# A hand-written interleaving of three pipelines: reciprocal before maximum on VectorE, and another order for TensorE's side work

## The chip, the cores and the metric

The kernel runs on 1 core of one Trainium2 chip. The metric is the device time of one execution in microseconds. Three runs of the kernel before took 1211.97 us in the median (1211.19 to 1215.45).

## The reference

The input is 8 sequences of 256 tokens with 256 channels, all in float32. Four layers follow one another, each with a residual and a layernorm (`x = _layernorm(x + layer(x))`):

- A: an operator with a long convolution. q, k and v are projected; q and k go through a depthwise convolution of 3 taps; `kv = k * v` is convolved over the sequence with `ssm_kernel` by FFT (here matrix products with a Fourier table); then `(y + kv * D_skip) * q` is projected.
- B: causal attention with 16 heads of 16 channels, whose output modulates a gated MLP of width 1024: `mod = 0.1 * tanh(attn @ A)`, `gate = silu(h @ W_in.T + mod * (h @ A) @ B)`, `mlp = gate * up @ W_down.T`.
- D: linear attention by a cumulative sum, `q * cumsum(k * v)`, and a projection.
- a mixture of 64 experts with 6 chosen per token, and a shared expert `silu(g) * u @ shared_down.T`. `topk` of the softmaxed router logits gives the weights.

The softmax of B is where the change is: for each head and each row of 256 scores the kernel takes the maximum, exponentiates with the sum collected on the way, takes the reciprocal of the sum, multiplies, and transposes the probabilities for the product with the values.

## The kernel before

The work has a first part, up to about 740 us, that runs the layers A, B and D (and the shared expert and the routing, called S and D4 to D6) over the 8 sequences, and then a loop over 133 chunks of 128 rows for the experts, and a last loop that adds the results up. The change touches only the first part.

That part is a software pipeline. In turn `it` layer A (and C, the preparation of B) works on sequence `it`, layer B on sequence `it - 1`, layer D on sequence `it - 2`, and the scattering of rows (G) on sequence `it - 3`. Each layer is cut into small parts with names, and a string of names (`TURN`, L313) gives their order. Every engine walks the same string in order and does its own share of each name, if it has one, so the string is the order of TensorE, VectorE, ScalarE and GpSimd at once. `TURN` is used in turns 0 and 2 to 7, `SECOND` in turn 1, `LAST_BUT_ONE` in turn 8 and `LAST` in turn 9. Semaphores alone hold the engines together; each engine is strictly in order.

Attention is cut into 12 units (0 to 3: four heads against 128 keys, 4 to 11: two heads against 256 keys). For unit u:

- TensorE's part `u` (L773) makes the scores of unit u (mask by L741, products by L744) into one of two banks, then transposes the probabilities of unit u-2 (`turn_probs`, L631, which waits for GpSimd's scaling of them and for ScalarE's copy of the transposes before), then multiplies those of u-3 with the values (L762; from unit 4 on two units together, L768, in every second part).
- VectorE's part (L1293) takes the maximum of unit u (L1301, wants the scores of u) and then the reciprocal of the sums of unit u-1 (L1307, wants the exponentials of u-1).
- ScalarE's part (L1012) exponentiates unit u (L1019, wants the maximum) and then copies the transposed probabilities of unit u-2 out of PSUM (L1025).
- GpSimd's part (L530) multiplies the probabilities of unit u-1 by the reciprocals (L537).

Between the units stand parts of A and D. Those the change moves: `A4b` (TensorE, L681, with L686: the second half of the inverse transform, 8 matmuls), `A4z` (VectorE, L1232: adds the skip term and multiplies by q, lines L1236 and L1243; it waits for A4b), `D3o` (VectorE, L1370: the layernorm's output x3, by L1163), `D4` (TensorE, L842: transposes x3 by L631, waits for D3o; ScalarE copies it out by L1063), `A5` (TensorE, L698: output projection of A, 8 matmuls by L626, waits for A4z), `A5n`, `A5o` (VectorE: residual, moments and output of A's layernorm), `S0` `S1` `S2` (TensorE L855/L864, ScalarE L1071/L1078, VectorE L1415/L1419 and L1422: the three tiles of the shared expert, each of which needs the one before to have left its PSUM bank), `SDa` and `SDb` (TensorE L883: the shared expert's output in two halves, both want S2's result), `SD` (VectorE L1451), `D4l` (TensorE L851: router logits), `D4m` (VectorE L1380 and ScalarE L1068), `A6n` (VectorE L1269 and L1272, GpSimd's root), `A6o` (VectorE L1277). In the trace x3 is named x_row. After unit 14 TensorE goes on with `B6c` (L787), the first instruction of a long stretch of MLP work.

Of the kernel before, what the change touches and what calls it, by code (L numbers as in the profile page):

```python
# [35 lines left out]
GROUPS = P // PAIR  # L36
# [85 lines left out]
def build(nc, d):  # L122
# [6 lines left out]
    with ExitStack() as ctx:  # L129
        def sb(name, shape, dt=F32):  # L130
            return ctx.enter_context(nc.sbuf_tensor(name, shape, dt))
# [64 lines left out]
        UNITS, PVS = GROUPS + 2 * GROUPS, 2 * GROUPS  # L196
        PROBS, PROBTS = 3, 4
        nmx, sums, rec = (sb(n, [P, UNITS, 4]) for n in ("nmx", "sums", "rec"))
# [77 lines left out]
        def need(eng, name, value):  # L276

            if isinstance(value, int) and value <= 0:
                return
            eng.wait_ge(S[name], value)  # L280
# [11 lines left out]
        class Chain:  # L292
# [17 lines left out]
                self.wait()  # L310


        TURN = """A1 A1b D1 A1q u0 D2k A1k u1 G0 D2x A2 u2 G1 D2v A3a u3 G2 A3b u4 G3 A3p D2q D2w u5 G4 D3 u6 G5 D3n A4a u7 G6 D3o D4 A4b A4z  # L313
            u8 G7 S0 u9 G8 A5 u10 G9 A5n D4l S1 u11 G10 A5o D4m S2 A6n u12 G11 SDa u13 A6o D4t SDb SD u14 B6a B6c B6b C1 f0 D4k f1 C2 f2 D5 f3 D5p C2v
            f4 D4w D5h f5 f6 f7 C2h B8 D6""".split()

        SECOND = """A1 A1b A1q A1k A2 A3a u0 A3b u1 A3p u2 u3 A4a u4 A4b A4z u5 u6 A5 u7 A5n u8 A5o u9 A6n u10 A6o u11 u12 u13 u14
# [10 lines left out]
        def turns(eng, parts):  # L328

            def turn(it, order=TURN):  # L330
                for name in order:
                    b = it - LAG[STAGE.get(name[0], name[0])]
                    if isinstance(b, int) and not 0 <= b < NB:
                        continue
                    if name in parts:
                        parts[name](b)
# [803 lines left out]
        def _(dve):  # L1140
# [152 lines left out]
            def unit(u):  # L1293
                w = P if u < GROUPS else L
                def part(b):
                    if u == 0:
                        cbn.start(b)
                    if u < UNITS:
                        dve.wait_ge(S["b_s"], b * UNITS + u + 1)
                        need(dve, "b_exp", (b - 1) * UNITS + u + 1)  # L1300
                        dve.tensor_reduce(nmx[:, u, 0:512 // w], bank[:, u % 2, :].rearrange("p (h k) -> p h k", k=w), AX, ALU.max,  # L1301
                                          negate=True).then_inc(S["b_max"], 1)
                    if u:
                        n = 4 if u - 1 < GROUPS else 2
                        dve.wait_ge(S["b_exp"], b * UNITS + u)
                        need(dve, "b_scaled", (b - 1) * UNITS + u)
                        dve.reciprocal(rec[:, u - 1, 0:n], sums[:, u - 1, 0:n]).then_inc(S["b_rec"], 1)  # L1307
                return part

            def B6(b):  # L1310
# [289 lines left out]
```

## Time and profile before

| | before |
|---|---|
| median of 3 runs | 1211.97 us (1211.19 to 1215.45) |
| the profiled execution's own time | 1210.18 us |
| its span | 1208.1 us |
| TensorE busy | 1030.5 us (85%) |
| VectorE busy | 690.0 us (57%) |
| GpSimd busy | 485.0 us (40%) |
| ScalarE busy | 360.7 us (30%) |

In a timeline a row gives the start in us, the time it took in us, the engine, the line, and what is written from what; in brackets stands how long the engine had been idle before it and what ended that. Matmuls overlap, so a row's end lies a little behind the next row's start. PE is TensorE, DVE is VectorE, ACT is ScalarE, POOL is GpSimd. Rows are merged where equal instructions follow one another (x8 are eight).

### The profile page before, as it was taken

To read this page: it belongs to the slowest core of one execution; us is meant where nothing else is said; L and a number is where in the kernel's file an instruction comes from. 1 tells how busy PE (TensorE), PEld (TensorE's weight loads), DVE (VectorE), ACT (ScalarE), POOL (GpSimd) and SP (SyncE) were. 2 spreads that over 40 slices of the span, in tenths; PEclk is the share of its full clock that TensorE was granted. 3 is DMA by queue.
4 is the path that set the end of the run, shared out by engine and by line. 5 is a ranking of instruction groups with operands and counts; after the bars stand their busy time and mean duration, and the time that the engine had idled before them with its cause. 6 is when DMAs were issued, how large, how long until landed. Compare 5 with 4: busy or idle time off the path is not lost. (4 is left out here: it accounts for less than half of the span.)

```text
span 1208.1 us, 23670 instructions
## 1 busy us (share of the span) xinstructions
PE 1030.5 (85%) x6301; PEld 841.4 (70%) x6301; DVE 690.0 (57%) x2250; ACT 360.7 (30%) x1114; POOL 485.0 (40%) x626
## 2 busy tenths in 40 slices
PE   5466798898998998997988888648999999999966
PEld 4344586776776776776866656537888888888955
DVE  1733455776765765675675646454555555555546
ACT  1024434344243243254253153001111111111243
POOL 0413224136245145154163152353555555555522
PEclk8778899999999999999999989968999999999989
DMA  9149950131220310410400410028999999999776
GB/s 363 62 101 290 286 124 1 40 88 37 75 62 31 90 45 35 104 32 31 104 29 25 104 37 19 29 92 268 308 307 309 306 302 302 306 291 310 263 259 245
DMA packets 129986, 184.67 MB, mean 153 GB/s; under 512 B 29749, under 2 KB 99989, under 8 KB 127517
## 3 DMA queue, kind: packets, MB, share of 16 engines
q1 hardware_dynamic: 94720, 104.41, 31.8%
q10 hardware_dynamic: 22989, 45.98, 11.0%
q0 software_dynamic: 12240, 33.83, 7.9%
q8 instruction: 18, 0.29, 0.1%
q14 instruction: 19, 0.16, 0.0%
HBM read 123.09 MB, written 61.60 MB: 153 GB/s over the span
## 5 line engine op out<-in xcount | busy, mean ns | idle before, releaser
L537 POOL TENSOR_TENSOR prob<-prob,rec 128x512 f32<-128x512 f32 x96 | 100.3, 1045 | 164.8 <-DVE rec L1307 163.4
L599 POOL DMA_INDIRECT y_rows<-sh_gu,ids x133 | 130.8, 984 | 60.2 <-POOL spare L290 56.8
L1019 ACT ACTIVATE prob<-bank,nmx 128x128 f32<-128x128 f32 (+1 forms) x256 | 104.9, 421 | 156.4 <-DVE nmx L1301 156.4
L1090 ACT ACTIVATE inv<-bank 88x256 f32<-88x256 f32 x159 | 60.3, 379 | 269.8 <-PE bank L929 269.8
L1523 DVE COPY sh_gu<-bank 128x256 f32<-128x256 f32 x133 | 56.4, 424 | 97.1 <-PE bank L938 96.8
L1301 DVE TENSOR_REDUCE nmx<-bank 128x2 f32<-128x512 f32 (+1 forms) x96 | 65.8, 686 | 77.4 <-PE bank L744 71.0
L938 PE MATMUL bank<-w_in,inv 88*128 88x256 f32 x428 | 109.8, 379 | 0.0
L631 PE MATMUL bank<-cst,prob 128*128 128x128 f32 x384 | 62.4, 287 | 39.3 <-ACT probT L1025 20.5
L562 POOL DMA_INDIRECT x_rows<-x_copy,desti x84 | 87.4, 1041 | 15.7 <-issue 15.7
L631 PEld LDWEIGHTS bank<-cst,prob 128*128 128x128 f32 x384 | 43.8, 146 | 55.3 <-POOL prob L537 50.6
L938 PEld LDWEIGHTS bank<-w_in,inv 88*128 88x128 f32 x428 | 72.7, 190 | 6.0
L802 PE MATMUL bank<-h2T,w_up 128*128 128x256 f32 x256 | 66.4, 382 | 0.0
L1025 ACT ACTIVATE probT<-bank 128x512 f32<-128x512 f32 x96 | 57.4, 598 | 28.8 <-PE bank L631 28.8
L804 PE MATMUL bank<-h2T,w_in 128*128 128x256 f32 x256 | 65.7, 379 | 0.0
L290 POOL TENSOR_TENSOR spare<-ones_row 128x1 f32<-128x1 f32 x168 | 31.1, 185 | 83.9 <-DVE sh_gu L1523 66.4
L815 PE MATMUL bank<-w_down,actT 128*128 128x256 f32 x256 | 60.0, 385 | 0.9
L929 PE MATMUL bank<-fwd,w_up 128*88 128x128 f32 x432 | 58.4, 279 | 2.4 <-DVE fwd L1505 1.5
L552 POOL TENSOR_TENSOR products<-z,products 128x512 bf16<-128x512 f32 x8 | 9.2, 1152 | 126.9 <-ACT products L1006 126.9
L929 PE MATMUL bank<-fwd,w_down 128*88 128x128 f32 x416 | 54.9, 275 | 2.4 <-DMA w_in<-in_e_w 1.3
L929 PE MATMUL bank<-inv,w_down 128*88 128x128 f32 x424 | 55.7, 274 | 1.0 <-DMA w_in<-in_e_w 0.3
L815 PEld LDWEIGHTS bank<-w_down,actT 128*128 128x128 f32 x256 | 46.8, 190 | 12.7 <-DVE actT L1329 6.3
L1046 ACT ACTIVATE gt<-bank 128x256 f32<-128x256 f32 x64 | 24.5, 383 | 104.0 <-PE bank L807 81.4
(264 smaller groups left out, 2300.0 us busy)
## 6 DMA issues: line engine op xcount, KB each, us to landing
w_in<-in_e_w ACTq DMA_DIRECT2D x107, 176.0 KB
w_down<-in_e_w SPq DMA_DIRECT2D x105, 176.0 KB
x_rows<-sgt SPq DMA_DIRECT2D x2, 8192.0 KB, 36.8
fwd<-x_rows SPq DMA_DIRECT2D x78, 132.0 KB
w_up<-in_e_w SPq DMA_DIRECT2D x54, 176.0 KB
w_up<-in_e_w ACTq DMA_DIRECT2D x52, 176.0 KB
w_down<-x_rows SPq DMA_DIRECT2D x54, 132.0 KB
stack_q<-q_parts SPq DMA_DIRECT2D x16, 384.0 KB, 6.0
```

Of the source, the lines that this page charges most:

```text
L537: pool.tensor_tensor(p, p, r, ALU.mult).then_inc(S["b_scaled"], 1)
L562: pool.indirect_dma_start(x_rows, bass.IndirectOffsetOnAxis(ap=desti[:, n:n + 1].bitcast(U32), axis=0), rows[:, n // TOPK, :], None).then_ ...
L599: pool.indirect_dma_start(y_rows, bass.IndirectOffsetOnAxis(ap=ids[s][:].bitcast(U32), axis=0), yc[s], None).then_inc(S[f"m_st{s}"], 16)
L631: return pe.transpose(out, x, ident)
L802: pe.matmul(psum(n, L, 2 * L), w_up[:, kt, cols], h2T[:, kt, :], start=(kt == 0), stop=(kt == KT - 1))
L804: pe.matmul(psum(n, 0, L), w_in[:, kt, cols], h2T[:, kt, :], start=(kt == 0), stop=False)
L815: mm = pe.matmul(psum(1, tt * D, (tt + 1) * D), actT[:, f, tt * P:(tt + 1) * P], w_down[:, f, :], start=(f == 0), stop=(f == FT - 1))
L929: mm = pe.matmul(bank[0:IH, 3 + n, m * P:(m + 1) * P], w1[s][:, kt, m * IH:(m + 1) * IH], xcT[n][:, kt, :], start=(kt == 0), stop=(kt == K ...
L938: mm = pe.matmul(psum(6 + c.slot(2), 0, D), hs[n][:, m, :], w2[s][:, m, :], start=(m == 0), stop=(m == 1))
L1019: i = act.activation(prob[:, u % PROBS, h * w:(h + 1) * w], psum(u % 2, h * w, (h + 1) * w), ACT.Exp, bias=nmx[:, u, h:h + 1], accum_out=s ...
L1090: act.activation(hs[n], bank[0:IH, 3 + n, 0:2 * P].rearrange("p (a b) -> p a b", a=2), ACT.Silu).then_inc(S["m_hs"], 1)
L1301: dve.tensor_reduce(nmx[:, u, 0:512 // w], bank[:, u % 2, :].rearrange("p (h k) -> p h k", k=w), AX, ALU.max, negate=True).then_inc(S["b_m ...
```

## The change

Two edits. In VectorE's part of a unit the reciprocal of unit u-1 now comes before the maximum of unit u. And in `TURN`, from unit 7 on, the side work stands in another order: A4b goes ahead of D4, D4 moves behind unit 8 and stands with A5, S0 moves behind unit 9, and SDa moves behind unit 13; VectorE's D3o now comes after A4z, and its A5n, A5o, D4m and A6n each come before the S part that they had followed. The other three orders stay.

```diff
-        TURN = """... A4a u7 G6 D3o D4 A4b A4z
-            u8 G7 S0 u9 G8 A5 u10 G9 A5n D4l S1 u11 G10 A5o D4m S2 A6n u12 G11 SDa u13 A6o D4t SDb SD u14 B6a ...
+        TURN = """... A4a u7 G6 A4b A4z D3o
+            u8 G7 D4 A5 u9 G8 A5n S0 u10 G9 D4l A5o S1 u11 G10 D4m A6n S2 u12 G11 A6o D4t u13 SDa u14 SDb SD B6a ...
@@ VectorE's unit(u) @@
+                    if u:
+                        n = 4 if u - 1 < GROUPS else 2
+                        dve.wait_ge(S["b_exp"], b * UNITS + u)
+                        need(dve, "b_scaled", (b - 1) * UNITS + u)
+                        dve.reciprocal(rec[:, u - 1, 0:n], sums[:, u - 1, 0:n]).then_inc(S["b_rec"], 1)
                     if u < UNITS:
                         dve.wait_ge(S["b_s"], b * UNITS + u + 1)
                         need(dve, "b_exp", (b - 1) * UNITS + u + 1)
                         dve.tensor_reduce(nmx[:, u, 0:512 // w], ...).then_inc(S["b_max"], 1)
-                    if u:
-                        ... (the same five lines)
```

## Rows read from the trace of the kernel before

**Rows 1.** The page: the span, and busy time with its share by engine.
```profile
span 1208.1 us, 23670 instructions
PE 1030.5 (85%) x6301; PEld 841.4 (70%) x6301; DVE 690.0 (57%) x2250; ACT 360.7 (30%) x1114; POOL 485.0 (40%) x626
```

**Rows 2.** Busy time by stretch: three TURN turns, each from L787 to L787.
```profile
core 0: us, PE busy (x) PEld busy (x) DVE busy (x) ACT busy (x) POOL busy (x), PEclk, DMA share, GB/s
221.24:307.21 85.97, 77.32 (x488) 61.58 (x484) 57.35 (x164) 34.02 (x109) 35.21 (x36) 1.00 0.23 60
...
483.57:570.51 86.94, 78.00 (x487) 61.34 (x483) 57.84 (x164) 34.01 (x109) 34.99 (x35) 1.00 0.22 58
570.51:659.18 88.67, 79.70 (x488) 62.49 (x484) 57.87 (x164) 34.01 (x109) 34.97 (x35) 0.98 0.20 54
```

**Rows 3.** Timeline of TensorE in a turn at full clock, unit 7 to B6c.
```profile
279.89 0.60 PE L631 MATMUL bank<-cst,prob 128*128 128x128 f32 x4
282.61 0.66 PE L631 MATMUL bank<-cst,x_row 128*128 128x128 f32 x4 [2.12 <-DVE x_row L1163]
283.10 1.89 PE L686 MATMUL bank<-inv,products 128*128 128x256 f32 x8
284.83 0.27 PE L741 MATMUL bank<-csb 128*128 128x256 bf16 x1
...
286.26 1.99 PE L864 MATMUL bank<-x3T,sh_gu 128*128 128x256 f32 x8
...
289.08 0.63 PE L631 MATMUL bank<-cst,prob 128*128 128x128 f32 x4 [0.49 <-ACT probT L1025]
...
292.40 0.63 PE L631 MATMUL bank<-cst,prob 128*128 128x128 f32 x4 [0.64 <-ACT probT L1025]
...
297.80 1.97 PE L864 MATMUL bank<-x3T,sh_gu 128*96 128x256 f32 x8 [0.62 <-DVE sact L1422]
300.04 0.63 PE L631 MATMUL bank<-cst,prob 128*128 128x128 f32 x4 [0.26 <-ACT probT L1025]
...
302.04 1.56 PE L883 MATMUL bank<-sh_dn,sact 128*128 128x256 f32 x6 [0.80 <-DVE sact L1422]
304.75 0.66 PE L631 MATMUL bank<-cst,prob 128*128 128x128 f32 x4 [1.15 <-POOL prob L537]
...
307.21 1.13 PE L787 MATMUL bank<-h2T,b_a 128*128 128x256 f32 x4
```

**Rows 4.** Timeline of VectorE in the same stretch.
```profile
280.95 1.61 DVE L1163 TENSOR_SCALAR x_row<-d_kv,mvD,yD 128x256 f32<-128x256 f32 x2
285.04 0.87 DVE L1236 SCALAR_TENSOR_TENSOR kv<-kv,vec,bank 128x256 f32<-128x256 f32 x2 [2.48 <-PE bank L686]
...
286.71 0.68 DVE L1301 TENSOR_REDUCE nmx<-bank 128x2 f32<-128x512 f32 x1
...
302.78 0.17 DVE L1307 RECIPROCAL rec<-sums 128x2 f32<-128x2 f32 x1
```

**Rows 5.** Timeline of GpSimd in the same stretch.
```profile
303.66 1.03 POOL L537 TENSOR_TENSOR prob<-prob,rec 128x512 f32<-128x512 f32 x1
```

**Rows 6.** Busy time by stretch, just behind D4's wait in two turns.
```profile
282.61:286.02 3.41, 3.41 (x31) 2.92 (x35) 0.87 (x2) 0.60 (x1) 0.68 (x1) 1.00 0.13 43
370.49:373.90 3.41, 3.41 (x11) 2.53 (x10) 0.57 (x2) 0.46 (x1) 0.00 (x0) 0.50 0.11 40
```

**Rows 7.** Timeline of TensorE in a turn with half clock: unit 9's transposes.
```profile
465.31 0.60 PE L631 MATMUL bank<-cst,prob 128*128 128x128 f32 x4
```

**Rows 8.** The tile rec: what VectorE and then TensorE waited for.
```profile
  ACT prob L1019: 4.8, 9
...
  PE bank L631: 18.5, 20
```

**Rows 9.** Timeline of VectorE at unit 2: its maximum, then unit 1's reciprocal.
```profile
262.93 0.69 DVE L1301 TENSOR_REDUCE nmx<-bank 128x4 f32<-128x512 f32 x1 [0.59 <-PE bank L744]
263.90 0.18 DVE L1307 RECIPROCAL rec<-sums 128x4 f32<-128x4 f32 x1 [0.28 <-ACT prob L1019]
```

**Rows 10.** Timeline of TensorE in turn 1 (SECOND), one of its unit steps.
```profile
126.58 0.63 PE L631 MATMUL bank<-cst,prob 128*128 128x128 f32 x4 [1.31 <-ACT probT L1025]
```

More of the change, by code:

```diff
@@ L310, in link @@
                 self.wait()
-        TURN = """A1 A1b D1 A1q u0 D2k A1k u1 G0 D2x A2 u2 G1 D2v A3a u3 G2 A3b u4 G3 A3p D2q D2w u5 G4 D3 u6 G5 D3n A4a u7 G6 D3o D4 A4b A4z
-            u8 G7 S0 u9 G8 A5 u10 G9 A5n D4l S1 u11 G10 A5o D4m S2 A6n u12 G11 SDa u13 A6o D4t SDb SD u14 B6a B6c B6b C1 f0 D4k f1 C2 f2 D5 f3 D5p C2v
+        TURN = """A1 A1b D1 A1q u0 D2k A1k u1 G0 D2x A2 u2 G1 D2v A3a u3 G2 A3b u4 G3 A3p D2q D2w u5 G4 D3 u6 G5 D3n A4a u7 G6 A4b A4z D3o
+            u8 G7 D4 A5 u9 G8 A5n S0 u10 G9 D4l A5o S1 u11 G10 D4m A6n S2 u12 G11 A6o D4t u13 SDa u14 SDb SD B6a B6c B6b C1 f0 D4k f1 C2 f2 D5 f3 D5p C2v
             f4 D4w D5h f5 f6 f7 C2h B8 D6""".split()
@@ L1302, in part @@
                                           negate=True).then_inc(S["b_max"], 1)
-                    if u:
[L1304 to L1307, printed above, removed]
                 return part
```

## The prediction

> **What bounds the kernel now.** I read the page first, then the busy time cut into turns, then the timeline of a whole turn on TensorE beside the other engines. The page says that TensorE is busy for 1030.5 of 1208.1 us and VectorE for 690.0 [rows 1]. Cut by turn, TensorE is busy for 77.3 of 86.0 us in a TURN turn, 90% [rows 2]. So such a turn is a queue of TensorE work with some holes, and only holes can be gained or lost. The six TURN turns with all layers in them take 85.6, 86.0, 88.3, 88.1, 86.9 and 88.7 us; three of them stand in [rows 2], the others are like them. The long ones show a granted clock of 0.98 and the two of 86.0 and 86.9 us show 1.00. The cause is seen in [rows 6]: behind the long wait of D4 the clock of TensorE was 0.50 (1.2 GHz) for 3.41 us in one turn, and 1.00 (2.4 GHz) in another. This happened in three of the six turns. The mean of the three long ones is 88.4 us, that of the two at 1.00 is 86.5 us: one such stretch costs 1.9 us.
>
> The holes between unit 7 and B6c are in [rows 3]: D4 waits 2.12 us for VectorE's x3; unit 9's part waits 0.49 and unit 10's 0.64 us for ScalarE's copy of transposes; S2 waits 0.62 us for the S1 tile; unit 12's part waits 0.26 us; SDa waits 0.80 us for the S2 tile; unit 13's part waits 1.15 us for GpSimd's scaling. A hole costs more than its bracket. Consecutive matmul rows overlap (282.61 + 0.66 lies 0.17 us behind 283.10), and the overlap is lost at a wait, so I add 0.17 for each.
>
> **Edit 1, the order in TURN.** I lay the new order out in the turn that begins its stretch at 280.33 (the end of the transposes in part u7, 279.89 + 0.60, less the overlap) [rows 3].
>
> A4b no longer waits behind D4. Its 8 matmuls take 1.73 us (283.10 to 284.83), so TensorE is in part u8 at 282.06. That part took 1.43 us (284.83 to 286.26), which gives 283.5. Now comes D4 and wants x3. VectorE was free early, and had x3 at 282.56 before (280.95 + 1.61). But D3o now stands behind A4z on VectorE, and A4z waits for A4b: its first row came 1.94 us after A4b's first matmul (283.10 to 285.04), so here at 282.27, and it occupied VectorE until the next maximum at 286.71, 1.67 us later [rows 4]. D3o therefore starts at 283.94, ends at 285.55, and D4 starts at 285.6 after a wait of 2.1 us. The wait that the eye goes to first is thus not removed; it moves behind unit 8. I cost it at no gain. With D3o ahead of A4z it would have gone.
>
> What goes are small waits behind it. D4 takes 0.49 and A5 1.73 us, unit 9's scores some 0.33: its transposes are wanted at 288.15. The maximum of unit 8 comes at 285.5, ScalarE's exponentials and copy follow in 2.2 us as they did before (the maximum at 286.71, the transposes at 289.08, 2.37 us), so the copy is there at 287.9 and the 0.49 us wait is gone. After S0 (1.84 us) unit 10's transposes are wanted at 290.8; unit 9's maximum comes at 288.44 with its scores, and 2.37 us later is 290.81, so the 0.64 us wait is gone, just. S1 starts at about 292.9. S2 came 3.32 us after S1's start and does so again, at 296.2, with the same 0.6 us wait. Unit 12's wait grows to about 0.35, as the reciprocal now precedes unit 11's maximum.
>
> SDa's 0.80 us wait is gone, since SDa stands behind unit 13 now. But it had covered part of unit 13's wait. Unit 11's reciprocal comes behind S2's tile on VectorE: S2's matmuls end at 298.2, D4m's exponentials and the tanh end about 299.1, the two VectorE rows of the tile 0.9 us later, at 300.0. A6n, which stood between (the reciprocal was at 302.78, 0.88 us after the tile), is past. The reciprocal takes 0.17 us and the scaling 1.03 [rows 4, 5], so the transposes can start at 301.35. TensorE is done with unit 12's part at 299.7: the wait is about 1.6 us instead of 1.15. Then 0.49 for the transposes, 1.4 for SDa, 0.58 for the values and 1.4 for SDb: B6c at 305.2 instead of 307.21. As a sum of waits: removed are 0.49 + 0.64 + 0.80 with three overlaps of 0.17, 2.44; added are 0.1 and 0.45; that makes 1.9 us a turn.
>
> This holds at full clock. In a half-clock turn unit 9's transposes had no wait before [rows 7], since TensorE was slow itself, so only 1.9 - 0.66, about 1.3 us, is to be had. Edit 1 gives 3 x 1.9 + 3 x 1.3 = 9.6 us. Bounds: all three removed waits come back in another place, 0; or also the added 0.55 does not come, 6 x 2.44 = 14.6. I take 9.6, since the walk rests on durations of the same instructions. No DMA is moved past anything: G stays with its unit, and SP's queue is not touched.
>
> **Edit 2, reciprocal first.** The reciprocal occupies VectorE for some 0.08 us ahead of each maximum (0.17 less overlap), 96 times. It can also hold the maximum back: where the exponentials of u-1 aren't ready when the scores of u are. Over the whole trace VectorE stood idle for the exponentials ahead of the reciprocal 9 times, 4.8 us [rows 8]. In those 9 places the maximum (0.61 us net) will come after that wait and not before it, some 1.1 us later. Unit 2 is one, in each turn: the maximum was at 262.93 and the reciprocal at 263.90 [rows 9], so the maximum now comes at about 264.0. Behind it D2v is held back by 0.6 us, and so unit 3's maximum and unit 4's transposes. Against it, the scaling of a unit starts 0.6 us earlier where VectorE comes with the scores. TensorE waited 18.5 us for scalings in all, 20 times [rows 8]; per turn these are unit 2's part (0.7), unit 6's (0.4) and unit 13's (1.15, which this edit doesn't reach, as S2's tile stands before it). I expect -0.6 and -0.4 for these, +0.7 for unit 4's part and +0.3 for what the later maxima add from unit 9 on: nothing, or 0.2 us lost, per turn. In turn 1, with little side work, TensorE waits for ScalarE's copies in most units [rows 10] and the maximum lies on that path: +0.1 us per unit at most. Turn 8 should gain some 0.5. Bounds: if every delay lay on the path, 96 x 0.08 + 9 x 1.1 = 18 us lost; if all waits for scalings but unit 13's went, 18.5 - 6 x 1.15, 12 us won. I take 1 us lost, nearest to the rows of a turn.
>
> **The sum.** 9.6 - 1 = 8.6 us. The expert loop behind starts that much earlier and does not change. From the profiled execution's 1210.2 this is 1201.6; the median of the runs is 1.8 above that execution, about one half-clock stretch. From 1211.97 it is 1203.4, and I forecast 1203.
>
> A rule that speaks to it: the small waits around units 9 to 13 (seven in 25 us) were all followed by a granted clock of 1.00 in the two turns without a half-clock stretch [rows 2, 3]. The Trainium skill, in "TensorE: Matmul & The Clock Gate", section "A second HAM failure mode: psum-queue depth-cycling", says that frequent short idle times between groups of matmuls can make the clock go back and forth. By that rule fewer holes would also lift the clock, and the sum would be near 1198; by the rows only the 2 us hole pulls it down, and it stays.
>
> **Rivals.**
> 1. The clock rises: D4's hole, now with more dense work around it, is no longer followed by half clock. 3 x 1.9 = 5.7 us more: 1197.5. For it: only three of six such holes did it before. Against: its length is the same. 12%.
> 2. The gain is taken back: unit 10's wait survives (its margin is 0.0 us) and unit 13's takes up more than 1.6, as it now stands behind S2's tile alone. 0.8 us left a turn, less edit 2: 1208. 20%.
> 3. Slower: the clock falls more often. The waits of units 12 and 13 (0.35 and 1.6 us, 1.1 us of work between them) form a second long hole. If half clock follows D4 in all six turns and unit 13 in five, 8 more stretches cost 15.2 us against 8.6: 1218.5. It decides from 4.5 more stretches on. Against: 0.80 and 1.15 us with SDa between them never did it. 5%.
> 4. Slower: the held-back maxima set the pace (18 us against 9.6): 1220. It decides once more than half of the delays are on the path. 3%.
>
> The forecast has 60%, its own range 1199.5 to 1207. The range for 8 in 10 reaches to rival 1 and most of rival 2: 1196 to 1210. Faster or slower begins at 0.5%, 6 us, what a measurement of this kernel can tell: faster (below 1205.9) is most of the forecast and rival 1, 0.70; same 0.24; slower 0.06.
>
> **What would show it.** Right: TURN turns of about 84 to 85 us at full clock; D4's row with a wait near 2 us behind unit 8; no bracket at the transposes of units 9 and 10 and at SDa; one of 1.5 us or more at unit 13; the maximum of unit 2 about 1 us later; as many half-clock stretches as now. Wrong: turns of 86 us, D4 without a wait, or half clock behind unit 13.

## The result, and the profile after

The changed kernel takes 1197.57 us (1196.18 to 1198.47, 4 runs) where the kernel before took 1212.33 us (1211.19 to 1215.45). The ratio is 0.9861, with a 95% interval of 0.9837 to 0.9886. That is 14.8 us less; 9 were forecast. On another chip, in a later run of the same kernel, the ratio was 0.9838 (0.9808 to 0.9869), 1194.37 against 1215.69 us. So the direction was right and the size was too small by a third or more.

The profiled execution, first the page (it answers to [rows 1]):

```profile
span 1196.5 us, 23670 instructions
PE 1029.0 (86%) x6301; PEld 841.4 (70%) x6301; DVE 680.5 (57%) x2250; ACT 361.4 (30%) x1114; POOL 484.8 (41%) x626
```

VectorE is busy for 9.5 us less (690.0 before) with the same 2250 instructions. The edits took no instruction away, so some of them became shorter: those that write x_row, D3o's, were busy for 11.7 us before and 6.6 after. That is the first sign of what the forecast missed.

The same cut into turns as in [rows 2], after; then turn 8, the stretch from there to the first expert chunk, and the rest:

```profile
219.68:302.85 83.17, 76.91 (x485) 61.72 (x484) 55.39 (x163) 34.06 (x109) 35.31 (x36) 1.00 0.23 62
472.79:556.96 84.17, 77.62 (x485) 61.47 (x483) 56.11 (x163) 34.06 (x109) 34.75 (x35) 1.00 0.23 60
387.01:472.79 85.78, 79.23 (x484) 62.52 (x483) 56.10 (x163) 34.06 (x109) 34.73 (x35) 0.98 0.23 59
...
641.12:719.91 78.79, 67.05 (x416) 51.66 (x414) 43.39 (x129) 30.88 (x101) 30.63 (x31) 0.94 0.23 61
719.91:803.72 83.81, 51.45 (x224) 39.57 (x221) 42.39 (x166) 8.59 (x19) 26.37 (x29) 0.81 0.17 56
803.72:1196.50 392.78, 364.76 (x2383) 319.28 (x2382) 210.35 (x906) 85.10 (x239) 197.24 (x334) 0.98 0.90 288
```

The stretches that answer to the last three, before:

```profile
659.18:739.24 80.06, 67.22 (x420) 51.71 (x416) 44.18 (x129) 31.07 (x102) 30.73 (x31) 0.94 0.23 60
...
739.24:821.01 81.77, 50.27 (x223) 38.75 (x220) 42.50 (x166) 8.57 (x19) 26.26 (x29) 0.83 0.17 57
821.01:1208.10 387.09, 361.19 (x2383) 318.58 (x2382) 208.38 (x906) 84.95 (x239) 196.36 (x334) 0.98 0.90 292
```

The comparable turns at full clock went from 86.9 to 84.2 and from 86.0 to 83.2 us, 2.8 each (1.7 forecast, edit 2's loss of 0.2 taken off). All six TURN turns together went from 523.5 to 504.6 us, 19.0 less. Of this 16.4 us is the gain at full clock, and 2.6 us comes from fewer half-clock stretches, one instead of three. Turn 8 gave 1.3. Against this stand 0.9 us up to B6c of turn 1, 2.0 us in turn 9, whose granted clock is lower (0.81 against 0.83; no run tests the cause), and 5.7 us in the expert loop and what follows. That makes the profile's 11.6. The loop's 5.7 is no effect of the change, as the runs below show.

The timeline of TensorE in the turn that answers to [rows 3]:

```profile
278.97 1.89 PE L686 MATMUL bank<-inv,products 128*128 128x256 f32 x8
...
281.20 0.63 PE L631 MATMUL bank<-cst,prob 128*128 128x128 f32 x4
281.76 0.65 PE L768 MATMUL bank<-probT,v 128*32 128x128 f32 x16
283.36 0.66 PE L631 MATMUL bank<-cst,x_row 128*128 128x128 f32 x4 [0.96 <-DVE x_row L1163]
283.86 1.89 PE L626 MATMUL bank<-a_wo,z 128*128 128x256 f32 x8
...
285.91 0.60 PE L631 MATMUL bank<-cst,prob 128*128 128x128 f32 x4
...
293.98 1.97 PE L864 MATMUL bank<-x3T,sh_gu 128*96 128x256 f32 x8 [0.62 <-DVE sact L1422]
296.27 0.63 PE L631 MATMUL bank<-cst,prob 128*128 128x128 f32 x4 [0.33 <-ACT probT L1025]
...
298.99 0.66 PE L631 MATMUL bank<-cst,prob 128*128 128x128 f32 x4 [1.51 <-POOL prob L537]
299.48 1.46 PE L883 MATMUL bank<-sh_dn,sact 128*128 128x256 f32 x6
...
302.85 1.03 PE L787 MATMUL bank<-h2T,b_a 128*128 128x256 f32 x4
```

The brackets of units 9 and 10 and of SDa are gone, S2 waits 0.62, unit 12 0.33 and unit 13 1.51 us, all as the forecast laid them out. One bracket is not: D4 waits 0.96 us, not 2.1. The cause is in VectorE's timeline, after (the answer to [rows 4]):

```profile
280.90 0.87 DVE L1236 SCALAR_TENSOR_TENSOR kv<-kv,vec,bank 128x256 f32<-128x256 f32 x2 [1.39 <-PE bank L686]
281.97 0.69 DVE L1243 TENSOR_TENSOR z<-kv,qc 128x512 f32<-128x512 f32 x1 [0.19 <-DVE kv L1236]
282.58 0.73 DVE L1163 TENSOR_SCALAR x_row<-d_kv,mvD,yD 128x256 f32<-128x256 f32 x2
```

D3o took 0.73 us; the same two instructions had taken 1.61 [rows 4]. GpSimd in these stretches, before and then after:

```profile
280.19 0.72 POOL L545 TENSOR_TENSOR yD<-vD,minus_half 128x2 f32<-128x2 f32 x1
281.02 1.04 POOL L537 TENSOR_TENSOR prob<-prob,rec 128x512 f32<-128x512 f32 x1
```

```profile
280.75 1.06 POOL L562 DMA_INDIRECT x_rows<-x_copy,desti  x1 [0.18 <-issue]
283.48 1.03 POOL L537 TENSOR_TENSOR prob<-prob,rec 128x512 f32<-128x512 f32 x1 [1.66 <-DVE rec L1302]
```

Before, D3o (280.95) ran beside a scaling (281.02 to 282.06) and ended 0.5 us behind it. After, D3o (282.58 to 283.31) found GpSimd idle.

### The profile page after: what moved, and what is told of

It reads as the page before. It is cut to its first block and busy times, and to the rows that moved or that the text cites. A ratio compares the mean times of both kernels' runs of the same rounds, so it can differ in the third digit from the quotient of the medians.

```text
span 1196.5 us, 23670 instructions
## 1 busy us (share of the span) xinstructions
PE 1029.0 (86%) x6301; PEld 841.4 (70%) x6301; DVE 680.5 (57%) x2250; ACT 361.4 (30%) x1114; POOL 484.8 (41%) x626
## 5 line engine op out<-in xcount | busy, mean ns | idle before, releaser
L929 PEld LDWEIGHTS bank<-fwd,w_up 128*88 128x88 f32 x432 | 50.4, 161 | 8.5 <-issue 5.8
```

The costliest lines, as they stand in the source:

```text
L929: mm = pe.matmul(bank[0:IH, 3 + n, m * P:(m + 1) * P], w1[s][:, kt, m * IH:(m + 1) * IH], xcT[n][:, kt, :], start=(kt == 0), stop=(kt == K ...
```

## The experiments

My theory was: the gain is edit 1's; the part of it that was missed is D3o's length, which depends on whether GpSimd works at the same time. Rivals were that the reciprocal's new place made the gain, that D3o is short for another reason, and that the expert loop gives back part of what is won.

**The two edits, each alone.** `e1_order_only` is the changed kernel with the maximum first:

```diff
                 def part(b):
-                    if u: ... reciprocal of u-1
                     if u < UNITS: ... maximum of u
+                    if u: ... reciprocal of u-1
```

> The changed kernel with VectorE's old order in a unit (maximum first, then reciprocal): the new order of the side work alone. My theory: the gain is all in the order, since D3o now runs beside an idle GpSimd (0.73 us instead of 1.61) and the small waits of units 9, 10 and SDa are gone. So: TURN turns of about 84 us at full clock, D3o at 0.73 us, D4's wait about 1 us, ratio to before 0.985 to 0.990. Rival (the reciprocal's place made the gain, by moving GpSimd's scalings out of D3o's way): D3o stays at 1.4 us or more, D4 waits about 2 us, and the ratio is 0.993 or above.

`e2_rec_only` is the kernel before with the same lines the other way round.

> The kernel before with the reciprocal ahead of the maximum: the other edit alone. My theory: worth nothing within 3 us, ratio 0.997 to 1.003: unit 2's and unit 6's waits for scalings shrink from 0.7 and 0.4 us to about 0.1 and 0, unit 4's wait grows to about 0.7. One thing could make it better: the scaling of unit 6 now starts before D3o; but GpSimd still has the root of D3n ahead of it, so D3o stays beside a scaling and takes 1.4 us or more. Rival (the edit is half of the gain): ratio 0.993 or below.

The order alone: 1195.12 us, ratio 0.9813 (0.9784 to 0.9841). The reciprocal's place alone: 1218.87 us, ratio 1.0022 (0.9996 to 1.0049). A full-clock turn and turn 8 of the first, by stretch:

```profile
384.71:468.47 83.76, 77.55 (x484) 61.45 (x483) 57.60 (x163) 33.89 (x109) 35.05 (x35) 1.00 0.23 60
636.01:716.76 80.75, 68.20 (x417) 52.49 (x415) 44.47 (x129) 30.80 (x101) 30.71 (x31) 0.92 0.23 60
```

The ratio of the first lies below the 0.985 to 0.990 that I expected. The order is worth 86.94 - 83.76 = 3.2 us a turn, and the reciprocal's place costs 0.4 of it (84.17 - 83.76). In turn 8 the changed kernel is 2.0 us shorter than this one (78.79 against 80.75), but at a granted clock of 0.94 against 0.92, so it is not shown how much of that is the reciprocal's own; without the new order turn 8 gained 0.5 us (80.06 to 79.57). The maximum of unit 2 is indeed late, as the forecast had it, 1.1 us later counted from B6c; VectorE in the changed kernel, where [rows 9] had the maximum 0.97 us ahead of the reciprocal:

```profile
262.31 0.18 DVE L1302 RECIPROCAL rec<-sums 128x4 f32<-128x4 f32 x1 [1.65 <-ACT prob L1019]
262.49 0.69 DVE L1306 TENSOR_REDUCE nmx<-bank 128x4 f32<-128x512 f32 x1
```

`e2_rec_only` showed something else. Its typical turn took 88.8 us, and half clock stood in five of its six turns, four times not behind D4 but behind the waits of SDa and unit 13. TensorE in one of them:

```profile
477.64 0.63 PE L631 MATMUL bank<-cst,prob 128*128 128x128 f32 x4 [0.33 <-ACT probT L1025]
478.20 0.64 PE L768 MATMUL bank<-probT,v 128*32 128x128 f32 x16
479.45 1.56 PE L883 MATMUL bank<-sh_dn,sact 128*128 128x256 f32 x6 [0.61 <-DVE sact L1422]
482.16 1.12 PE L631 MATMUL bank<-cst,prob 128*128 128x128 f32 x4 [1.15 <-POOL prob L537]
483.07 2.69 PE L883 MATMUL bank<-sh_dn,sact 128*128 128x256 f32 x6
```

The transposes behind the third wait take 1.12 us and the six matmuls 2.69, where they take 0.66 and 1.46 at full clock. So three waits of 0.33, 0.61 and 1.15 us, with work between them, can have half clock behind them. They need not: the kernel before has nearly the same three there, 0.26, 0.80 and 1.15 us [rows 3], and no half clock behind them in any of its six turns.

**D3o beside GpSimd, and behind it.** Both runs are the changed kernel with one more multiply of GpSimd:

```diff
+            def beside(b):
+                pool.wait_ge(S["a_zq"], b + 1)      # e5: S["d_x3"], under the name D3o
+                one = ones_row[:].rearrange("p (o l) -> p o l", o=1).broadcast_to([P, KT, L])
+                pool.tensor_tensor(h1T[:], one, one, ALU.mult)
-            turns(pool, {"A3p": A3, ...
+            turns(pool, {"A4z": beside, "A3p": A3, ...
```

> The changed kernel, and GpSimd makes one more multiply of 128x512 (about 1.05 us, of ones into a tile that is dead then) that starts as A4z's product is done, so beside D3o. It computes nothing that is used. My theory (the same VectorE instruction takes twice as long while GpSimd works on SBUF): D3o takes 1.4 us or more instead of 0.73, D4's wait grows from 0.96 to 1.7 to 2.0 us, each full-clock TURN turn is 0.7 to 1.0 us longer, 4 to 6 us in all above the changed kernel (1202 us), more if half-clock stretches come back. Rival (D3o is short because of its place behind A4z, or because of what TensorE does, not because of GpSimd): D3o stays at 0.73 us and the time within 1 us of the changed kernel.

> Control for the run with GpSimd's extra multiply beside D3o: the same multiply, but it waits for D3o's result, so it runs just behind it and beside unit 8's maximum, which reads PSUM. My theory: D3o stays at 0.73 us, D4's wait at 0.96 us, the maximum at 0.67 to 0.69 us, unit 7's scaling comes 1.1 us later, which TensorE doesn't notice (it has 1.3 us in hand), and the time is within 1.5 us of the changed kernel. Rival (any extra work on GpSimd costs, since it holds up the scalings): the same 4 to 6 us as in the other run.

With the multiply beside D3o: 1202.66 us, ratio 0.9867 (0.9831 to 0.9902). Behind it: 1194.41 us, 0.9806 (0.977 to 0.9843). The three engines in the first:

```profile
282.06 1.45 DVE L1168 TENSOR_SCALAR x_row<-d_kv,mvD,yD 128x256 f32<-128x256 f32 x2
...
282.24 1.13 POOL L592 TENSOR_TENSOR h1T<-ones_row 128x512 f32<-128x512 f32 x1 [0.97 <-DVE z L1248]
...
283.57 0.66 PE L636 MATMUL bank<-cst,x_row 128*128 128x128 f32 x4 [1.68 <-DVE x_row L1168]
```

and in the second:

```profile
283.22 0.73 DVE L1170 TENSOR_SCALAR x_row<-d_kv,mvD,yD 128x256 f32<-128x256 f32 x2
...
284.04 1.03 POOL L594 TENSOR_TENSOR h1T<-ones_row 128x512 f32<-128x512 f32 x1 [1.60 <-DVE x_row L1170]
...
284.00 0.66 PE L638 MATMUL bank<-cst,x_row 128*128 128x128 f32 x4 [0.96 <-DVE x_row L1170]
```

The same work of GpSimd costs 0.7 us of D3o and 0.72 us of D4's wait when it lies beside D3o, and nothing when it comes just behind. The overlap with D3o and not the load on GpSimd is the cause. The times of the two runs differ by 8.3 us, more than six times 0.72. In the profiled executions the six turns differ by 6.0 us, one half-clock stretch among them; the rest lies outside the turns.

VectorE is not slowed evenly: in the first run D3o's second instruction started at 282.38 and ended at 283.51, 0.14 us behind GpSimd's end. That reads as if it stood still until GpSimd was done, and another pair, in `e9_both`, bears it out. There D3o starts 0.06 us behind GpSimd's multiply and takes 1.47 us; this pair starts 0.42 us behind one and takes 1.10:

```profile
451.88 1.10 DVE L1163 TENSOR_SCALAR X<-qc,mvA,yA 128x256 f32 x2
...
451.46 1.04 POOL L537 TENSOR_TENSOR prob<-prob,rec 128x512 f32<-128x512 f32 x1 [0.34 <-DVE rec L1302]
```

In the traces of all the runs a `tensor_scalar` of 128x256 overlaps a multiply of GpSimd 408 times. In 338 of them it was held up, and whatever its start, from 0.86 us behind GpSimd's to 0.08 us ahead of it, it ended 0.14 to 0.16 us behind GpSimd's end. In 69 of the others it had started 0.16 us or more ahead and kept its 0.33 to 0.41 us.

**The same cure in the kernel before.** `e6_before_waits` leaves every order as it was, and lets GpSimd's scaling of unit 6 wait for D3o:

```diff
+                    if u == 6:
+                        need(pool, "d_x3", b)
                     pool.wait_ge(S["b_rec"], b * UNITS + u + 1)
```

> The kernel before, where only GpSimd's scaling of unit 6 also waits for D3o's result. D3o then runs beside GpSimd's idleness. My theory: D3o takes 0.73 us instead of 1.61, D4's wait falls from 2.12 to about 1.25 us, and TensorE does not miss the scaling, which it wants 2.5 us later: 0.9 us less a turn, and fewer half-clock stretches behind D4 (three before, 1.9 us each): 5 to 10 us less, ratio 0.991 to 0.996. Rival (D3o's length isn't what D4's wait hangs on, or GpSimd's work is delayed onto the path): no gain or a loss.

It measured 1208.41 us, ratio 0.9927 (0.9901 to 0.9952). VectorE, TensorE and GpSimd in one of its turns:

```profile
541.21 0.74 DVE L1165 TENSOR_SCALAR x_row<-d_kv,mvD,yD 128x256 f32<-128x256 f32 x2
...
542.01 0.66 PE L633 MATMUL bank<-cst,x_row 128*128 128x128 f32 x4 [1.25 <-DVE x_row L1165]
...
542.11 1.04 POOL L539 TENSOR_TENSOR prob<-prob,rec 128x512 f32<-128x512 f32 x1 [0.93 <-DVE x_row L1165]
```

D3o took 0.72 to 0.74 us in each TURN turn, D4 waited 1.25 us in five of the six, and a turn at full clock took 86.11 us (86.94 before). Half clock stood behind unit 13 in two turns and behind D4 in none.

**What the forecast said of D3o's place.** `e3_x3_first`:

```diff
-            A4a u7 G6 A4b A4z D3o
+            A4a u7 G6 A4b D3o A4z
```

> The changed kernel with VectorE's D3o ahead of A4z instead of behind it; nothing else. By my forecast's reading D4's wait (0.96 us) would go. D3o would start about 279.6 in a turn's time, beside the scaling of unit 6 and so at 1.6 us, and end before A4b does or 0.3 us behind it; A4z is 0.3 us late; x3 is there 1.2 us before TensorE reaches D4. Expected: no wait at D4, TURN turns 0.9 to 1.1 us shorter, ratio to before 0.981 to 0.984. Rival (the time of GpSimd beside D3o is what counts, wherever it stands): D3o slows and is late all the same, gain under 0.3 us a turn.

1190.45 us, ratio 0.9803 (0.9765 to 0.984). D4 waited for nothing, though D3o took 1.48 us, beside a scaling. Turns at full clock took 83.2 us, 1.0 less, as expected.

**Unit 13's wait.** `e8_s2_behind` gives VectorE's share of S2 a name of its own, V2, and puts it behind unit 12 (also in the last two orders); `e7_sda_back` puts SDa ahead of unit 13 again:

```diff
-            D4m A6n S2 u12 G11 A6o D4t u13 SDa u14      (changed kernel)
+            D4m A6n S2 u12 V2 G11 A6o D4t u13 SDa u14   (e8)
+            D4m A6n S2 u12 G11 SDa u13 A6o D4t u14      (e7)
```

> The changed kernel, with VectorE's share of S2 (its two tile rows) moved behind its share of unit 12, so that unit 11's reciprocal doesn't wait for the S2 tile; the same in the last two orders. Expected: the 1.51 us wait at unit 13's transposes is gone or under 0.3 us; SDa then wants S2's tile at about the time it is ready (0 to 0.4 us of wait). TURN turns 1.2 to 1.6 us shorter, ratio to before 0.978 to 0.981, and no half-clock stretch behind unit 13. Rival (the wait only moves on to SDa): the turns stay within 0.4 us.

> The changed kernel with SDa back ahead of unit 13. By the forecast's sum that part of the new order is worth little: SDa's wait (0.4 to 0.8 us and an overlap) comes back, unit 13's wait falls from 1.51 to 0.3 us or less, since SDa's 1.4 us of work cover it. Expected: a turn within 0.5 us of 84.2, the sum of the two waits 0.8 to 1.6 us. Rival (SDa behind unit 13 is one of the edit's main gains, as the kernel before had 0.80 + 1.15 us here): turns 0.5 us or more longer than 84.2.

`e8_s2_behind`: 1189.29 us, 0.9777 (0.9743 to 0.981); `e7_sda_back`: 1191.89 us, 0.983 (0.9785 to 0.9875). A full-clock turn took 83.36 and 83.73 us. The first is less than I expected: unit 13 still waited 0.70 us, as GpSimd made A6n's root ahead of the scaling.

```profile
461.57 0.72 POOL L545 TENSOR_TENSOR yR<-vR,minus_half 128x2 f32<-128x2 f32 x1
462.27 1.03 POOL L537 TENSOR_TENSOR prob<-prob,rec 128x512 f32<-128x512 f32 x1
...
463.35 0.66 PE L631 MATMUL bank<-cst,prob 128*128 128x128 f32 x4 [0.70 <-POOL prob L537]
```

The second says that SDa's move was by itself a loss of 0.4 us a turn, too little to stand out in the times of the runs (1187.51 to 1200.29 us, and 1193.92 to 1200.63 for the changed kernel on the same chip): with SDa back, its wait was 0.27 us, unit 13's was gone, and unit 14's values waited 0.69 us.

**Both, and what is left.** `e9_both` has e3's and e8's lines together; `e11_max_first` is the same with the maximum first; `e12_both_x3_alone` is e9 with e6's wait on GpSimd; `e10_after_again` is the changed kernel unchanged.

> Both corrections together: D3o ahead of A4z and S2's tile behind unit 12's reciprocal. If TensorE's holes in a turn are independent, the gains add: 2.1 to 2.7 us a turn, 13 to 16 us in all before what the expert loop gives back; ratio to before 0.970 to 0.976. Rival (the expert loop, whose weight transfers run at about 96% of the DMA engines, gives back what comes earlier): the first part ends 13 to 16 us earlier but the time falls by less than 8 us.

> The changed kernel once more, unchanged, on the chip of the next three. Its first measurement was 0.9861 of before, and the order alone 0.9813 on another chip, where the kernel before ran at 1216.5 us instead of 1212.3. My theory: the two differ by edit 2's 0.35 us a turn and by how often the clock was halved, so here it comes to 0.981 to 0.986, with turns of 84.2 us at full clock and 0 to 2 half-clock stretches in the six TURN turns. Rival: edit 2 costs 5 us in the new order, and the ratio is again 0.986 or more.

> The fastest so far (D3o ahead of A4z, S2's tile behind unit 12's reciprocal), with VectorE's old order in a unit: maximum first. In the TURN turns edit 2 cost 0.35 us each, in turn 8 it won 2 us (78.8 against 80.8). Expected: turns of 81.9 to 82.2 us instead of 82.4, turn 8 2 us longer, the whole within 1.5 us of the fastest so far (ratio 0.971 to 0.974). Rival (edit 2 helps once the other holes are gone): 2 us or more slower.

> The fastest so far, where GpSimd's scaling of unit 6 also waits for D3o's result, so that D3o runs beside an idle GpSimd again (0.73 us instead of 1.47). In the kernel before this was worth 0.9 us a turn, as D4 waited for D3o. Here D4 waits for nothing. My theory: D3o falls to 0.73 us and the turns stay at 82.4 us within 0.2, since nobody waits for it: the contention costs only where its victim is waited for. Rival (contention on SBUF costs in itself): 0.5 us or more a turn faster.

| kernel | us | ratio (95%) | full-clock turn | turn 8 |
|---|---|---|---|---|
| e9_both | 1182.30 | 0.9724 (0.9692 to 0.9755) | 82.37 | 77.61 |
| e10_after_again | 1194.37 | 0.9838 (0.9808 to 0.9869) | 84.2 | 78.6 |
| e11_max_first | 1185.72 | 0.976 (0.9731 to 0.9789) | 82.84 | 79.67 |
| e12_both_x3_alone | 1182.03 | 0.9722 (0.9694 to 0.975) | 82.74 | 78.0 |

`e9_both` beats both `e3_x3_first` and `e8_s2_behind`: the two gains add in a turn (84.17 - 82.37 = 1.8, against 1.0 and 0.8). I had expected 2.1 to 2.7, as `e8_s2_behind` was not yet measured. In `e11_max_first` I had expected turns 0.3 us shorter and they were 0.5 longer: with the other holes closed, the scalings that come late with the maximum first (waits of 2.47 us a turn for them, 1.36 in `e9_both`) are what TensorE meets. In `e12_both_x3_alone` D3o fell to 0.73 us and the turn did not get shorter, since D4 did not wait for it any more. It got 0.4 us longer, as GpSimd's scaling, held back for D3o, now comes late: TensorE waits 0.38 us for it.

The last stretch of the kernel, from the first expert chunk to the end, in `e10_after_again`, `e9_both` and `e8_s2_behind`:

```profile
806.76:1192.40 385.64, 359.95 (x2383) 319.23 (x2382) 207.31 (x906) 85.10 (x239) 196.38 (x334) 0.98 0.91 293
```

```profile
788.78:1176.30 387.52, 361.31 (x2383) 318.58 (x2382) 208.73 (x906) 84.95 (x239) 196.39 (x334) 0.98 0.90 292
```

```profile
795.12:1192.60 397.48, 368.09 (x2383) 319.16 (x2382) 211.72 (x906) 85.10 (x239) 197.22 (x334) 0.97 0.90 284
```

The changed kernel's own stretch is 392.78 us in one execution and 385.64 in another, and `e9_both`, which enters it 32 us earlier than the kernel before, needs 387.5 against 387.1. The loop gives nothing back; its length varies by up to 12 us between executions of these kernels, with the transfer rate (284 to 293 GB/s). Why the rate varies is open.

## Why the prediction was right or wrong

**The holes of edit 1: right.** Units 9 and 10 and SDa lost their waits, unit 12 and 13 came to 0.33 and 1.51 us (0.35 and 1.6 forecast), and S2 stayed. The maximum of unit 2 came about 1 us later, as forecast. D4's wait and the number of half-clock stretches did not come as forecast.

**The step that failed: "D3o therefore starts at 283.94, ends at 285.55".** The forecast's start is right relative to A4b (3.61 us after its first matmul; 3.61 measured), but the length, 1.61 us, was taken from the one place where D3o stood before and carried to a place where GpSimd is idle. There it is 0.73. With that number the same walk gives 24.0 us from A4b to B6c, and 23.88 were measured (24.87 forecast). This is 0.88 of a turn's missing 1.1 us; e4, e5 and e6 show that the length is GpSimd's doing. So the term that was mis-sized is D4's wait, which stood in the sum at 2.1 us and no gain: it measured 0.96. The trace of the kernel before had it, in the least, the middle and the greatest duration of these instructions in ns:

```profile
L1163 DVE TENSOR_SCALAR x_row<-d_kv,mvD,yD x16: 392/422/1269, 195.4 to 783.6; 128x256 f32<-128x256 f32 x16
```

And in its chain of waits these two instructions stand with 0.73 us in turn 9, where GpSimd made no multiply (it issued a transfer from 783.40 on, which did them no harm):

```profile
783.25 0.73 DVE x_row L1163 x2
```

The Trainium skill states the mechanism in "SBUF — State Buffer", "SBUF: two separate sides": VectorE and GpSimd share one pair of SBUF ports, as an exclusive lock that one of them holds for a whole instruction. Its section "Who interferes with whom" counts `tensor_scalar` among the operations that can need the pair. The traces agree: the held-up instruction ended 0.14 us behind GpSimd's multiply. The Trainium skill says in the same two sections that the first to start gets the pair. Here that holds from 0.16 us on; in [rows 4] D3o started 0.07 us ahead of GpSimd by the record and was still the one that waited.

With D3o at 0.73 us the forecast's own sum would have been 6 x 0.88 = 5.3 us lower, an estimate of 1197.7. That this is the measured 1197.57, and rival 1's 1197.5 too, is luck: 2.6 us more came from the clock and 1.3 from turn 8, and turns 1 and 9 and the expert loop took 8.6 back, all in the profiled execution.

**"By the rows only the 2 us hole pulls it down, and it stays": wrong.** Half-clock stretches went from three to one in the six turns (0 to 2 in the other kernels with the new order). D4's hole, now 0.96 us, has none behind it, nor has it in `e4_gpsimd_beside`, where it is 1.68 us. And smaller waits can do it: behind the cluster of SDa and units 12 and 13 half clock stood in 4 turns of `e2_rec_only`, 2 each of `e3_x3_first`, `e4_gpsimd_beside` and `e6_before_waits`, and 1 each of the changed kernel's two profiles and of `e5_gpsimd_behind`. In the four kernels in which no wait of the cluster is over 0.7 us (`e7_sda_back`, `e8_s2_behind`, `e9_both`, `e12_both_x3_alone`) it stood in none of 24 turns. But it also stood in none of the 18 turns of the kernel before, `e1_order_only` and `e11_max_first`, where unit 13 waits 1.0 to 1.75 us. What decides it stays open. The rule that the forecast quotes from the Trainium skill, "TensorE: Matmul & The Clock Gate", section "A second HAM failure mode: psum-queue depth-cycling", that frequent short idle times can make the clock go back and forth, fits these turns better than the forecast's own; no run here tests it by itself.

The price of a stretch was too high as well. The forecast's 1.9 us sets the long turns against the mean of 86.0 and 86.9, but the first of these belongs to a turn that is 1.0 us shorter than the later ones in the changed kernel too (83.17 against 84.17). Against 86.94 the three long turns cost 1.1 to 1.7 us; in the changed kernel it was 1.6 (85.78 - 84.17). Two smaller readings: the small waits that the forecast counts as seven are six, the seventh being D4's, and one of its half-clock turns, the last, did keep unit 9's wait of 0.49 us.

**Edit 2: the sign right, the size near.** 0.4 us lost per turn at full clock (0.2 forecast) and 0.9 in turn 1. Turn 8 won 0.5 us in `e2_rec_only`, as forecast, and 2 us beside the new order, with a higher granted clock. By itself the edit can't be told from nothing, ratio 1.0022. What I had not seen is that its sign turns with its surroundings: it wins 0.5 us a turn once D4's hole is closed and unit 13's is reduced.

**Rivals.** The first (the clock rises) came true in part, for another reason: D4's hole did not keep its length. Of the third, half clock behind unit 13 happened in one turn of six, and the kernel was not slower for it. The second and the fourth did not happen.

## What to carry to other kernels

A duration belongs to a place: before an instruction is moved, look up its minimum and maximum in the trace and what the other engines do beside each, above all GpSimd for a `tensor_scalar` of VectorE with SBUF operands. When you ask what the clock will do, look not at the longest wait alone: clusters of shorter ones had half clock behind them here, in some turns and not in others, so a forecast should give that a chance of its own. And an edit that neither wins nor costs anything is worth measuring again once the holes beside it are closed, for its sign may change.

## What the runs showed of the hardware

- A pair of `tensor_scalar` of 128x256 (f32, SBUF to SBUF) takes 0.73 us beside an idle GpSimd and, as D3o, 1.44 to 1.61 us beside a GpSimd multiply of 128x512; what is held up ends 0.14 to 0.16 us behind GpSimd's end; the maximum over PSUM beside the same multiply kept its 0.67 us. GpSimd's multiply lengthened little: 1.13 us in `e4_gpsimd_beside`, 1.03 in `e5_gpsimd_behind`.
- TensorE's granted clock fell to half behind idle times of 0.33, 0.61 and 1.15 us within 5 us, the longest of them shorter than D4's 2 us, in 4 of 6 turns of `e2_rec_only`; behind idle times of 0.26, 0.80 and 1.15 us it stayed at full in the 6 turns of the kernel before.
- The last part of the kernel, with its DMA engines busy for 90% of the time, took 385.6 to 397.5 us in executions that do the same work there.
